# State-space stage of a MetaFormer kernel: GpSimd weighs two tiles per operation, and makes its u tiles as neighbouring pairs

## The reference, cut to what matters

```
dt  = softplus(dt @ dt_w.T + dt_b)
A   = -exp(A_log)
dA  = exp(dt[..., None] * A)
dBx = dt[..., None] * Bm[:, :, None, :] * xc[..., None]
h   = dA_t * h + dBx_t                    # scan over the 576 positions, 16 states per channel
y   = einsum('bds,bs->bd', h, C_t)        # sum over the states
y   = (ys + xc * D) * silu(z) @ out_w.T
```

## Time and profile before

| | us |
|---|---|
| median of 3 runs | 966.7 (965.54 to 967.24) |
| the profiled execution, its own time | 964.93 |
| its span in the profile | 963.1 |
| busy PE, DVE, ACT, POOL | 790.4, 704.1, 369.9, 515.5 |

### The profile page before, as it was taken

The page is one execution under the profiler, slowest core; times in us unless marked ns, Lnnn a source line. Parts: engine busy times, 40 slices in busy tenths (PEclk is TensorE's granted clock), DMA queues, the critical chain, the costliest instruction groups (busy, mean ns, idle before and its releaser), DMA issues. The chain is left out here.

```text
span 963.1 us, 18898 instructions
## 1 busy us (share of the span) xinstructions
PE 790.4 (82%) x7645; PEld 487.0 (51%) x7657; DVE 704.1 (73%) x911; ACT 369.9 (38%) x557; POOL 515.5 (54%) x403
## 2 busy tenths in 40 slices
PE   8888888889998757878877887878887887788696
PEld 4555554556664534545554555545554545455464
DVE  4985985550004018999999999999999898975798
ACT  1220002123333575455555555455655454321000
POOL 5000000000000018999999999999999998970043
PEclk9999998999998977999999999999999998899688
DMA  4000000000000134666676667666666666510001
GB/s 145 4 5 5 4 5 1 1 0 1 1 0 2 50 112 137 194 193 190 192 213 197 189 187 215 196 193 191 191 210 199 174 194 199 175 47 1 0 0 50
DMA packets 55352, 102.68 MB, mean 107 GB/s; under 512 B 11200, under 2 KB 12352, under 8 KB 55264
## 3 DMA queue, kind: packets, MB, share of 16 engines
q1 hardware_dynamic: 55072, 100.74, 34.4%
q0 software_dynamic: 192, 0.72, 0.2%
HBM read 97.87 MB, written 3.54 MB: 105 GB/s over the span
## 5 line engine op out<-in xcount | busy, mean ns | idle before, releaser
L495 POOL TENSOR_TENSOR ring<-ring,big 128x576 f32<-128x576 f32 x206 | 284.8, 1403 | 18.1 <-DVE ring L865 11.8
L179 PE MATMUL banks<-ring,main_params 128*128 128x288 f32 x824 | 248.6, 432 | 4.6 <-POOL ring L495 2.8
L865 DVE TENSOR_TENSOR_SCAN ring<-big,banks 128x576 f32<-128x576 f32 x154 | 202.6, 1340 | 2.3
L179 PEld LDWEIGHTS banks<-ring,main_params 128*128 128x128 f32 x824 | 149.4, 196 | 61.6 <-POOL ring L495 15.3
L853 DVE TENSOR_TENSOR banks<-banks,big 128x576 f32<-128x576 f32 x192 | 143.0, 745 | 29.9 <-PE banks L1173 27.5
L472 POOL COPY big<-normed 128x576 f32<-128x576 f32 x4 | 2.7, 666 | 297.9 <-DVE normed L372 297.9
L672 ACT ACTIVATE big<-big,small 128x576 f32<-128x576 f32 x192 | 142.2, 764 | 27.3 <-DVE ring L865 21.5
L1172 PE MATMUL banks<-big,selectors 96*128 96x512 bf16 x192 | 74.8, 391 | 77.7 <-DVE ring L865 36.7
L979 PE MATMUL banks<-big 32*32 32x288 f32 x3968 | 102.3, 422 | 19.0 <-issue 15.6
L672 ACT ACTIVATE banks<-big,small 128x576 f32<-128x576 f32 x64 | 47.4, 741 | 112.6 <-DVE ring L865 89.8
L979 PEld LDWEIGHTS banks<-big 32*32 32x32 f32 x3968 | 62.4, 103 | 53.8 <-issue 33.8
(11 more groups left out here) (170 smaller groups left out, 1068.2 us busy)
## 6 DMA issues: line engine op xcount, KB each, us to landing
big<-bc_rows SPq DMA_DIRECT2D x640, 144.0 KB, 3.1
bc_rows<-big SPq DMA_DIRECT2D x16, 144.0 KB, 2.4
residual<-x_in SPq DMA_DIRECT2D x4, 288.0 KB, 7.7
out<-big SPq DMA_DIRECT2D x2, 512.0 KB, 3.1
main_params<-main_in SPq DMA_DIRECT2D x1, 895.0 KB, 9.8
big<-front_in POOLq DMA_DIRECT2D x1, 574.5 KB, 7.7
experts<-experts_in SPq DMA_DIRECT2D x1, 512.0 KB, 10.5
main_params<-main_in SPq DMA_DIRECT2D x1, 158.0 KB, 2.8
```

The costliest lines, as they stand in the source:

```text
L179: last = nc.tensor.matmul(PS[rows, 2 * p + a, 0:HALF], lhsT, rhs[:, bass.ds(at + a * HALF, HALF)], start=start, stop=stop, skip_group_chec ...
L495: nc.gpsimd.tensor_tensor(slot, slot, CT[n % 10], ALU.mult).then_inc(weighted, 1)
L865: nc.vector.tensor_tensor_scan(slot, DECAY[m % 3], place, 0.0, ALU.mult, ALU.add).then_inc(scanned, 1)
```

## The change

C rows are loaded two at a time into five double buffers, B rows of POOL_U tiles two at a time into two double buffers. GpSimd weighs a pair of neighbouring tiles (2k, 2k + 1) by one 128x1152 operation at n = 2k + 2, and POOL_U is now (6, 7, 14, 15), whose u tiles are made in pairs by one operation on two B rows, with DTX repeated, at n % 16 == 4 and 12. The gate and the additions come one step later.

```diff
-        CT = [big(L) for _ in range(10)]
-        BT = [big(L) for _ in range(3)]
+        CT = [big(2 * L) for _ in range(5)]
+        BT = [big(2 * L) for _ in range(2)]
...
-        SLOT = [RING[:, i * L:(i + 1) * L] for i in range(8)] + MORE
+        SLOT_PAIR = [RING[:, 2 * i * L:2 * (i + 1) * L] for i in range(4)] + [MORE]
+        SLOT = [t[:, i * L:(i + 1) * L] for t in SLOT_PAIR for i in range(2)]
...
-        POOL_U = (3, 7, 11, 15)
+        POOL_U = (6, 7, 14, 15)
...
-            def spread_row(dst, b, w, s, loaded):
+            def spread_rows(dst, b, w, s, count, loaded):
 
                 for d in range(2):
-                    sp.dma_start(dst[d * DI:(d + 1) * DI, :],
-                                 BCD[b, w, d, s].unsqueeze(0).to_broadcast([DI, L])).then_inc(loaded, 16)
+                    rows = BCD[b, w, d, s:s + count].rearrange("s t -> (s t)")
+                    sp.dma_start(dst[d * DI:(d + 1) * DI, :], rows.unsqueeze(0).to_broadcast([DI, count * L])).then_inc(loaded, 16)
...
-                if n >= 10:
-                    sp.wait_ge(weighted, n - 9)
-                spread_row(CT[n % 10], b, 1, s, c_loaded[n % 10])
-                if s in POOL_U:
-                    m = POOL_TILES.index(n)
-                    if m >= 3:
-                        sp.wait_ge(u_pool, m - 2)
-                    spread_row(BT[m % 3], b, 0, s, b_loaded[m % 3])
+                if s % 2 == 0:
+                    k = n // 2
+                    if k >= 5:
+                        sp.wait_ge(weighted, k - 4)
+                    spread_rows(CT[k % 5], b, 1, s, 2, c_loaded[k % 5])
+                if s in POOL_U and s % 2 == 0:
+                    m = POOL_TILES.index(n) // 2
+                    if m >= 2:
+                        sp.wait_ge(u_pool, m - 1)
+                    spread_rows(BT[m % 2], b, 0, s, 2, b_loaded[m % 2])
...
             def inputs_on_pool(n):
-                m = POOL_TILES.index(n)
-                pool.wait_ge(b_loaded[m % 3], 32 * (m // 3 + 1))
+
+                m = POOL_TILES.index(n) // 2
+                pool.wait_ge(b_loaded[m % 2], 32 * (m // 2 + 1))
                 pool.wait_ge(dtx_set, n // DS + 1)
-                wait_slot(pool, n)
-                nc.gpsimd.tensor_tensor(SLOT[n % SLOTS], BT[m % 3], DTX[n // DS % 2], ALU.mult).then_inc(u_pool, 1)
-
-            def weigh(n):
-                pool.wait_ge(scanned, n + 1)
-                pool.wait_ge(c_loaded[n % 10], 32 * (n // 10 + 1))
-                slot = SLOT[n % SLOTS]
-                nc.gpsimd.tensor_tensor(slot, slot, CT[n % 10], ALU.mult).then_inc(weighted, 1)
+                wait_slot(pool, n + 1)
+                nc.gpsimd.tensor_tensor(two(SLOT_PAIR[n // 2 % 5]), two(BT[m % 2]),
+                                        DTX[n // DS % 2].unsqueeze(1).to_broadcast([128, 2, L]), ALU.mult).then_inc(u_pool, 1)
+
+            def weigh(k):
+
+                pool.wait_ge(scanned, 2 * k + 2)
+                pool.wait_ge(c_loaded[k % 5], 32 * (k // 5 + 1))
+                slots = SLOT_PAIR[k % 5]
+                nc.gpsimd.tensor_tensor(slots, slots, CT[k % 5], ALU.mult).then_inc(weighted, 1)
...
-                if n >= 1:
-                    weigh(n - 1)
-                if n + AHEAD in POOL_TILES:
+                if n >= 2 and n % 2 == 0:
+                    weigh(n // 2 - 1)
+                if n + AHEAD in POOL_TILES and n % 2 == 0:
                     inputs_on_pool(n + AHEAD)
...
-                    dve.wait_ge(u_pool, POOL_TILES.index(n) + 1)
+                    dve.wait_ge(u_pool, POOL_TILES.index(n) // 2 + 1)
...
-                if n >= DS and n % DS == 3:
+                if n >= DS and n % DS == 4:
                     gate_image(n // DS - 1)
...
-                pe.wait_ge(weighted, n + 1)
+                pe.wait_ge(weighted, n // 2 + 1)
                 pair_matmul(Y_PAIR, par("ident"), SLOT[n % SLOTS], 0, start=False, stop=s == DS - 1).then_inc(y_added, 1)
 
-            ADDS = [[-3], [-2], [-1], [], [0], [1, 2]] + [[s - 3] for s in range(6, DS)]
-            for n in range(-AHEAD, NTILES + 3):
+            ADDS = [[-4], [-3], [-2], [-1], [], [], [0, 1], [2, 3]] + [[s - 4] for s in range(8, DS)]
+            for n in range(-AHEAD, NTILES + 4):
```

More of the change, by code:

```diff
@@ L132, in build_program @@
         TMP = [big(L) for _ in range(2)]
-        MORE = [big(L) for _ in range(2)]
+        MORE = big(2 * L)
         pos[0] = 0
@@ L214, in build_program @@
         rows_stored = [sem(f"rows_stored{i}") for i in range(3)]
-        c_loaded = [sem(f"c_loaded{i}") for i in range(10)]
-        b_loaded = [sem(f"b_loaded{i}") for i in range(3)]
+        c_loaded = [sem(f"c_loaded{i}") for i in range(5)]
+        b_loaded = [sem(f"b_loaded{i}") for i in range(2)]
         sp_step, sp_set, dt_set, dtx_set = sem("sp_step"), sem("sp_set"), sem("dt_set"), sem("dtx_set")
@@ L480, in step_sizes, with two @@
                     pool.wait_ge(u_dve, (b - 1) * (DS - len(POOL_U)))
-                    pool.wait_ge(u_pool, (b - 1) * len(POOL_U))
+                    pool.wait_ge(u_pool, (b - 1) * len(POOL_U) // 2)
                 nc.gpsimd.tensor_tensor(DTX[b % 2], DT[b % 3], image(XC, b), ALU.mult).then_inc(dtx_set, 1)
+            def two(t):
+                return t.rearrange("p (i t) -> p i t", i=2)
             def inputs_on_pool(n):
-                m = POOL_TILES.index(n)
-                pool.wait_ge(b_loaded[m % 3], 32 * (m // 3 + 1))
+                m = POOL_TILES.index(n) // 2
+                pool.wait_ge(b_loaded[m % 2], 32 * (m // 2 + 1))
                 pool.wait_ge(dtx_set, n // DS + 1)
-                wait_slot(pool, n)
-                nc.gpsimd.tensor_tensor(SLOT[n % SLOTS], BT[m % 3], DTX[n // DS % 2], ALU.mult).then_inc(u_pool, 1)
-            def weigh(n):
-                pool.wait_ge(scanned, n + 1)
-                pool.wait_ge(c_loaded[n % 10], 32 * (n // 10 + 1))
-                slot = SLOT[n % SLOTS]
-                nc.gpsimd.tensor_tensor(slot, slot, CT[n % 10], ALU.mult).then_inc(weighted, 1)
+                wait_slot(pool, n + 1)
[6 more added lines that the diff above has]
+                nc.gpsimd.tensor_tensor(slots, slots, CT[k % 5], ALU.mult).then_inc(weighted, 1)
             step_sizes(0)
             for n in range(-AHEAD, NTILES + 1):
-                if n >= 1:
-                    weigh(n - 1)
-                if n + AHEAD in POOL_TILES:
+                if n >= 2 and n % 2 == 0:
+                    weigh(n // 2 - 1)
+                if n + AHEAD in POOL_TILES and n % 2 == 0:
                     inputs_on_pool(n + AHEAD)
```

## The result

The changed kernel takes 1049.9 us (median of 4 runs, 1047.8 to 1051.6) against 966.3 us: a ratio of 1.0863 (95% interval 1.084 to 1.0887), 8.6% slower. Forecast were 1038 us and a range of 1000 to 1054. The profiled execution took 1051.6 us.

What follows compares the result with a forecast made beforehand. GpSimd was taken as the bound at 30.87 us an image, VectorE 2 us behind. A 32.5 us chain plus a 3.45 us TensorE wait gave 36.0 us an image, 72 us more in all: 1038 us, range 1000 to 1054.

Steps and rivals of the forecast that it cites:

- The size and the price: GpSimd's two-tile operation takes 2.62 us; two single ones cost 2.73, so a merge saves 0.155 us.
- The chain: Scans 6 and 14 wait for a weighing, then the u pair: 16.27 us per half, 32.5 us an image.
- TensorE's queue and its clock: bc_rows behind moved additions delays the product of tile 12 by 1.25 us, 3.45 at low clock: 36.0 us an image.
- the sign: VectorE's products waiting for a TensorE spread, 3 us at tile 12.
- The low stretch of the burst: TensorE's D*x and additions after 4.3 us without work: 4.5 us at the low clock, losing 2.2 us.
- the rival at 0.12: TensorE's clock falls in both halves: + 15, 1053 us; chance 0.12, shared with dearer operations (1046 to 1066).
- The sum: State-space stage: last gate at 936.2 us, 72 us behind 863.97, which gives a time of 1038 us.
- Costed at nothing: Loads landing 3.1 us after issue, the store of rows, ScalarE's decays, the moved gate and step_sizes: no cost in the stage.
- the cover I named: B rows of a pair stand in SP's queue some 10 us ahead of their u; landing over 8 us would delay it.

Runs made afterwards that it cites:

- u first: Changed kernel with GpSimd making the u pair before the weighing that stood ahead of it, at n % 16 == 4 and 12; 1012.2 us, ratio 1.0472.
- with u(7) and u(15) out of the way: Changed kernel with each u pair made by two 128x576 operations, each with its own signal, weighings still in pairs; 1018.4 us, ratio 1.0522.
- a run put right: Changed kernel with the additions and the gate where they stood before the change, GpSimd's part as changed; 1032.0 us, ratio 1.068.

## Why the prediction was right, point by point

- **The size and the price.** 2.62 us per two-tile operation forecast, 2.624 and 2.628 measured, and 2.58 us to the next start (614.74 to 617.32). A merge saves 0.15 us. The Trainium skill (GPSIMD Engine Reference, Performance versus the Vector engine) would by my estimate give 0.06; the row decides for 0.15. That the saving doesn't show in the time is a matter of the chain.
- **The chain.** 32.5 us forecast; 16.31 us for a half in the trace, waits of 1.58 and 2.24 us where 1.6 and 2.3 were. That it is the cause: without the order (u first) 38 us less, with u(7) and u(15) out of the way 31.5 less.
- **TensorE's queue and its clock.** 3.45 us an image forecast, all between scan 6 and scan 14, and 36.28 - 32.6 = 3.7 measured, but made up otherwise. That half is 18.7, 19.4 and 19.6 us long by turns, 2.4 to 3.3 us over the chain's 16.3, so the forecast was too high there. Its wait is spread over the products of tiles 9, 11 and 12, and 1.01 us of it is left at tile 12, where I had named 3 us as the sign. The start of that product was foreseen well: 11.3 to 12.2 us behind scan 6, where the sum had 12.35. The low stretch of the burst was 3.2 and 4.6 us in the two images looked at, where I took 4.5. The other half, in which I had no wait, was 16.3, 17.4 and 17.8 us long. The clock falls in both halves, as the rival at 0.12 had it, though with no wait behind it in every third image. That the image comes out within 0.3 us of 36.0 is in part luck: one half was put too high by about as much as the other was put too low. The Trainium skill (TensorE: Matmul & The Clock Gate, What's actually happening) has activity release the throttle; the trace agrees, with a low clock after 4.18 empty us and a granted clock of 0.99 again in 638:640 once work had resumed at 634.84.
- **The sum.** 72.2 us more in the stage forecast, 581.3 - 502.8 = 78.5 measured. 8.2 us more stand ahead of the stage, where I had nothing. So the rival's 1053 us is nearer to the 1049.9 than my 1038 only by these; in the stage alone its 87 us are 9 too many and my 72 are 6 too few.
- **Costed at nothing.** The loads landed after 4.6 us and not 3.1, without a wait in the changed kernel; the cover I named went as soon as u came earlier (1.27 us in the kernel with u first). For the gate and step_sizes no wait in the stage shows. The decays of ScalarE, also costed at nothing, are named as what ended four of the waits at scans 6 and 14 (7.0 us), but these are no longer than the others (1.57 and 2.24 us).
- **The step that a run put right** is one of the expectations: I took the moved additions for a loss that can be undone, and expected 45 us of it. It was 18, and nothing once u came first.

## What to carry to other kernels

Where two engines feed each other with 2 us of slack an image, a larger operation has to be read as a later first result: what it delays (the second input's signal, the first tile's weighing) is worth more than its fixed cost, here 0.15 us against waits of 1.6 and 2.2. Put what someone waits for ahead of what nobody does, and split what has two readers. And look where the matmul engine goes empty by the new order: its clock is part of the chain.

## What was not expected of the hardware

The stretch ahead of the stage has the same code in all fourteen kernels, but its first scan starts between 359.5 and 371.0 us after the span's start. Measured at the same VectorE instructions, the changed kernel is 3.2 us behind the kernel before at 83 us, 4.2 at 261 us and 8.2 at 357 us. The waits of TensorE's weight loads from 296 to 366 us, in the changed kernel and then in the kernel before, show one part of it:

```profile
PEld banks L1125 <- issue: 4.5, 3, 3.7
```

```profile
PEld banks L1116 <- issue: 1.8, 9, 0.4
```

A single pause of 3.7 us, in which TensorE waits for nothing that the profile shows, is most of the last 4 us. What makes it was not tried; it is why the table has a column for the stage.

Also: nine zero matmuls, 1.3 us of them per image, made the kernel before, in which TensorE isn't the bound, faster by 0.4%.
